# Cross attention: the low parts and the doubling of a tile's packed keys go from VectorE to GpSimd

## The chip, the core and the metric

The kernel runs on one core of one Trainium2 chip. The metric is the device time of one execution in microseconds (us); several runs are taken and their median is given. In the text PE is TensorE, DVE is VectorE, ACT is ScalarE, POOL is GpSimd and SP is the engine that issues the transfers from HBM.

## The reference

The program computes a small network of six layers on x of shape (2, 128, 256) with a context of shape (2, 2048, 256). The change lies in the first layer, a cross attention with 32 heads of 8 numbers:

```python
    k_raw = context @ Wk.T
    v_raw = context @ Wv.T
    ...
    q = _rmsnorm(q)
    k = _rmsnorm(k)
    scale = HEAD_DIM ** (-0.5)
    scores = jnp.einsum('bhnd,bhmd->bhnm', q, k) * scale
    attn = jax.nn.softmax(scores, axis=-1)
    out = jnp.einsum('bhnm,bhmd->bhnd', attn, v)
```

The fourth layer needs a weighted sum over the same context (a decaying scan whose mean is taken), so the kernel weighs each context tile while it is on the chip. The other layers (self attention, two feed-forward layers, a phase layer, experts) come afterwards and are not touched.

## The kernel before, in words

**Tiles.** The context is cut into 32 tiles of 128 rows (16 for each of two batches; `NB` is 32, `MB` is 16). Each tile t goes through the same steps on all engines, and a slot of most buffers is used by every second tile (`t % 2`).

**The way of a tile's keys.** POOL splits the context tile into an f16 high part and an f16 low part (`split_context`, lines L1694 and L1696). PE projects it into PSUM bank 7 (`project`, L1855). DVE takes the keys (`take_k`, L1563) and the values (`take_v`, L1570) out. POOL squares the keys (`square_keys`, L1687), DVE sums the squares of each head (`mean_squares`, L1576), ACT makes the reciprocal root by a logarithm and an exponential (`key_rstd`, L1795 and L1797). Then DVE makes the packed keys in `pack_keys`: the normalised keys `kn` (L1583), their f16 high part (L1590), the low part, that is `kn` minus the high part (L1592), and a doubling copy of 128x512 f16 (L1595). PE transposes the packed keys into bank 7 (`turn_keys`, L1867), DVE takes them out (`take_keys`, L1602). They are then used for the scores (L1884), ACT takes exponentials of the scores (L1805, four for each tile), and PE multiplies with the values (L1897).

**Weighing.** POOL multiplies each context tile with the decay weights (L1707) and adds the product to a sum (L1709) in `weigh_context`; for the first tile of a batch it is one multiplication (L1704).

**Order.** Each engine runs its own instruction list in the order in which the code is written, and semaphores join the lists. In its loop over t, DVE takes keys and values of tile t + 2, sums its squares, takes the transposed keys of tile t + 1, and then packs the keys of tile t + 2. POOL squares the keys of tile t, splits the context tile t + 2 and weighs tile t. For the second batch's queries POOL does some more at tiles 7 to 11 (`norm_q1` L1717, `high_q1` L1722, `low_q1` L1726), behind the weighing of the tile. SP loads a context tile into one of four slots when the weighing of four tiles before has freed it.

The buffers `kn` (128x256 f32, one slot), `kpack` (f16, two slots) and `ksq` are parts of the tile that the profile calls `sb_big`; `kraw`, `krs`, `kms` and the context tiles are parts of `sb_arena`; the split context lies in `sb_w_ri`.

Of the kernel before, what the change touches and what calls it, by code (L numbers as in the profile page):

```python
# [16 lines left out]
ALU = mybir.AluOpType  # L17
# [9 lines left out]
XH, XD = 32, 8  # L27
# [29 lines left out]
def build_program(nc, io):  # L57
    ctx = ExitStack()
    with ctx:
        sems = {}  # L60

        def sem(name):
            if name not in sems:
                sems[name] = ctx.enter_context(nc.semaphore(name))
            return sems[name]
# [87 lines left out]
        kn = big[:, 12800:13056]  # L153
        kpack = big[:, 13056:14080].bitcast(F16).rearrange("p (s n) -> p s n", s=2)
# [41 lines left out]
        for name, _, _ in loads:  # L196
            loaded[name] = loaded.get(name, 0) + 16
# [1293 lines left out]
        def pool_rest(pool):  # L1491
            G = nc.gpsimd
            pool_attention(pool)
            pool.wait_ge(sem("w_phase"), loaded["w_phase"])
            pool.wait_ge(sem("attn_out"), B)
            pool.wait_ge(sem("xf_low"), B)
            for kt in range(KT):
                for w in range(CONV):
                    G.tensor_tensor(w_cm[:, kt, w], w_mem[:, kt], w_conv[:, w], ALU.mult).then_inc(sem("w_cm_ready"), 1)
            for b in range(B):  # L1500

                pool.wait_ge(sem("summary_added"), b + 1)
                G.tensor_tensor(x[:, b], x[:, b], vecs[:, 2], ALU.add).then_inc(sem("beta_added"), 1)
            pool_scaled_units(pool)
            pool_phase(pool)
            pool_experts(pool)

        @block.vector
        def _(dve):
            V = nc.vector  # L1510
# [68 lines left out]
            def pack_keys(t):  # L1579

                dve.wait_ge(sem("k_rstd"), t + 1)
                knb = kn.rearrange("p (h d) -> p h d", d=XD)
                V.tensor_tensor(knb, kraw[:, t % 2].rearrange("p (h d) -> p h d", d=XD),  # L1583
                                krs[:, t % 2, :, None].to_broadcast([P, XH, XD]), ALU.mult
                                ).then_inc(sem("k_normed"), 1)
                if t >= 2:
                    dve.wait_ge(sem("k_transposed"), t - 1)
                dve.wait_ge(sem("k_normed"), t + 1)
                pack = kpack[:, t % 2].rearrange("p (h s r d) -> p h s r d", s=2, r=2, d=XD)
                V.tensor_copy(pack[:, :, 0, 0], knb).then_inc(sem("k_high"), 1)  # L1590
                dve.wait_ge(sem("k_high"), t + 1)
                V.tensor_tensor(pack[:, :, 0, 1], knb, pack[:, :, 0, 0], ALU.subtract).then_inc(sem("k_low"), 1)  # L1592
                dve.wait_ge(sem("k_low"), t + 1)
                halves_of = kpack[:, t % 2].rearrange("p (h s c) -> p h s c", s=2, c=16)
                V.tensor_copy(halves_of[:, :, 1], halves_of[:, :, 0]).then_inc(sem("k_packed"), 1)  # L1595

            def take_keys(t):

# [24 lines left out]
            take_v(0)  # L1623
            pack_q(0)
            pack_keys(0)
            mean_squares(1)
            take_keys(0)
            pack_keys(1)
            for t in range(NB):
                if t + 2 < NB:  # L1630
                    take_k(t + 2)
                    if t + 2 not in ACT_VALUES:
                        take_v(t + 2)
                    if t + 2 < MB:
                        decay_weights(t + 2)
                    else:
                        sum_weights(t + 2 - MB)
                    mean_squares(t + 2)
                if t + 1 < NB:
                    take_keys(t + 1)  # L1640
                if t + 2 < NB:
                    pack_keys(t + 2)
                if t == 4:
                    mean_squares_q(1)
# [36 lines left out]
        @block.gpsimd  # L1681
        def _(pool):
            G = nc.gpsimd

            def square_keys(t):
                pool.wait_ge(sem("k_taken"), t + 1)
                G.tensor_tensor(ksq[:, t % 2], kraw[:, t % 2], kraw[:, t % 2], ALU.mult).then_inc(sem("k_squared"), 1)  # L1687

            def split_context(t):

                pool.wait_ge(sem(f"ctx_loaded{t % CTX_SLOTS}"), 16 * (t // CTX_SLOTS + 1))
                if t >= 2:
                    pool.wait_ge(sem("kv_projected"), t - 1)
                G.tensor_copy(ctx_half[:, t % 2, 0], ctxT[:, t % CTX_SLOTS]).then_inc(sem("ctx_high"), 1)  # L1694
                pool.wait_ge(sem("ctx_high"), t + 1)
                G.tensor_tensor(ctx_half[:, t % 2, 1], ctxT[:, t % CTX_SLOTS], ctx_half[:, t % 2, 0],  # L1696
                                ALU.subtract).then_inc(sem("ctx_split"), 1)

            def weigh_context(t):

                pool.wait_ge(sem("geo_ready"), min(t + 1, MB))
                g = geo[:, None, (t % MB) * P:(t % MB + 1) * P].to_broadcast([P, KT, P])
                if t % MB == 0:
                    G.tensor_tensor(uacc[:, t // MB], ctxT[:, t % CTX_SLOTS], g, ALU.mult).then_inc(sem("ctx_weighted"), 1)  # L1704
                    return
                pool.wait_ge(sem("ctx_weighted"), t)
                G.tensor_tensor(gprod[:], ctxT[:, t % CTX_SLOTS], g, ALU.mult).then_inc(sem("ctx_weighed"), 1)  # L1707
                pool.wait_ge(sem("ctx_weighed"), t - t // MB)
                G.tensor_tensor(uacc[:, t // MB], uacc[:, t // MB], gprod[:], ALU.add).then_inc(sem("ctx_weighted"), 1)  # L1709

            qn1 = xn[:, 1].rearrange("p (h d) -> p h d", d=XD)
            pack1 = qpack[:, 1].rearrange("p (h s r d) -> p h s r d", s=2, r=2, d=XD)

            def norm_q1():
                pool.wait_ge(sem("q_rstd"), 2)
                pool.wait_ge(sem("q_copied"), 2)
                G.tensor_tensor(qn1, qraw[:, 1].rearrange("p (h d) -> p h d", d=XD),  # L1717
                                qrs[:, 1, :, None].to_broadcast([P, XH, XD]), ALU.mult).then_inc(sem("q1_normed"), 1)

            def high_q1(r):  # L1720
                pool.wait_ge(sem("q1_normed"), 1)
                G.tensor_copy(pack1[:, :, 0, r], qn1).then_inc(sem("q1_high"), 1)  # L1722

            def low_q1(r):
                pool.wait_ge(sem("q1_high"), r + 1)
                G.tensor_tensor(pack1[:, :, 1, r], qn1, pack1[:, :, 0, r], ALU.subtract).then_inc(sem("q1_packed"), 1)  # L1726

            split_context(0)
            split_context(1)
            weigh_context(0)  # L1730
            split_context(2)
            weigh_context(1)
            split_context(3)
            for t in range(2, NB):
                square_keys(t)
                if t + 2 < NB:
                    split_context(t + 2)
                weigh_context(t)
                if t == TURN_AT - 6:
                    norm_q1()  # L1740
                if TURN_AT - 5 <= t < TURN_AT - 3:
                    high_q1(t - TURN_AT + 5)
                if TURN_AT - 3 <= t < TURN_AT - 1:
                    low_q1(t - TURN_AT + 3)
            pool_rest(pool)
# [313 lines left out]
```

## Time and profile before

| | us |
|---|---|
| median of 3 runs | 408.24 |
| lowest and highest of them | 407.40, 408.91 |
| the profiled execution | 406.9 |
| its span, first to last instruction | 405.3 |
| PE, DVE, ACT, POOL busy in the span | 374.2, 329.2, 267.6, 221.5 |

The span is what the rows of a trace add up to; 1.6 us of the execution lie outside of it. The profiled execution is a single one, 1.3 us below the median of the three timed runs. A busy engine need not be the one that sets the end: PE is counted busy while its pipelined products drain.

### The profile page before, as it was taken

What the parts mean: (1) busy time and instruction counts of PE and PEld (TensorE: products, weight loads), DVE (VectorE), ACT (ScalarE), POOL (GpSimd) and SP (SyncE); (2) the same over time, 40 slices, a digit from 0 to 9 for tenths busy, and PEclk for the clock granted to TensorE, in tenths of its full rate; (3) what the DMA queues carried; (4) which work ended last, traced back from release to release, by engine and by line L of the source; (5) the groups of instructions that cost most, each with busy time, mean ns of one, the idle gap of its engine ahead of it and who ended that gap; (6) DMA issues with size and microseconds to landing.
All of it is one profiled execution on the core that took longest, in us unless ns stands there. A gap on an engine that the chain in (4) does not pass through costs nothing.

```text
span 405.3 us, 14183 instructions
## 1 busy us (share of the span) xinstructions
PE 374.2 (92%) x5863; PEld 288.4 (71%) x5863; DVE 329.2 (81%) x736; ACT 267.6 (66%) x554; POOL 221.5 (55%) x286
## 2 busy tenths in 40 slices
PE   7889989999999999889999999989889987799996
PEld 4456656666666767679989897778778864567775
DVE  7788989997799998768999996787997677866663
ACT  3588888897988898975545533822999246345532
POOL 2566577766566666016544430630399746999500
PEclk9999999999999999999999999999999999999999
DMA  5647641652311100570000017120000391000000
GB/s 165 234 136 247 225 140 44 185 158 69 113 40 38 35 25 4 158 287 2 2 0 2 1 46 313 32 112 1 2 2 2 123 392 62 2 1 2 2 0 27
DMA packets 10832, 34.77 MB, mean 86 GB/s; under 512 B 2193, under 2 KB 7313, under 8 KB 8977
## 3 DMA queue, kind: packets, MB, share of 16 engines
q1 hardware_dynamic: 10624, 33.86, 24.3%
q8 instruction: 47, 0.77, 0.7%
q14 instruction: 17, 0.13, 0.1%
q10 hardware_dynamic: 144, 0.00, 0.0%
HBM read 33.60 MB, written 0.26 MB: 84 GB/s over the span
## 4 chain that ended last, share of the span: by engine, by line
PE 51%; DVE 23%; POOL 10%; issue 9%; ACT 4%; DMA 1%; SPq 0%; DVEq 0%; POOLq 0%; ACTq 0%
PE ps L1897 9%; PE ps L1264 6%; PE ps L1855 5%; PE ps L1246 5%; PE ps L1884 3%; PE ps L1867 3%; PE ps L975 3%; PE ps L957 3%; PE ps L473 2%; PE ps L916 2%; POOL sb_w_ri L1696 2%; PE ps L923 2%; ACT sb_arena L1805 2%; DVE sb_big L654 2%; PE ps L534 1%
## 5 line engine op out<-in xcount | busy, mean ns | idle before, releaser
L1805 ACT ACTIVATE sb_arena<-ps 128x1024 f32<-128x1024 f32 x128 | 123.7, 1019 | 12.1 <-PE ps L1884 11.7
L1897 PE MATMUL ps<-sb_arena 128*25 128x128 f32 (+1 forms) x2048 | 68.7, 274 | 0.3 <-ACT sb_arena L1805 0.3
L1897 PEld LDWEIGHTS ps<-sb_arena 128*25 128x25 f32 (+1 forms) x2048 | 50.3, 97 | 7.5 <-ACT sb_arena L1805 1.0
L1855 PE MATMUL ps<-sb_w_ri 128*32 128x512 f16 x768 | 47.3, 379 | 3.0 <-DVE sb_arena L1602 1.8
L563 POOL TENSOR_TENSOR sb_halves<-sb_big,sb_halves 128x256 fp32r<-128x256 f32 x28 | 21.6, 792 | 43.7 <-ACT sb_halves L547 43.7
L1687 POOL TENSOR_TENSOR sb_big<-sb_arena 128x256 f32<-128x256 f32 x30 | 18.7, 623 | 45.3 <-DVE sb_arena L1563 45.3
L1855 PEld LDWEIGHTS ps<-sb_w_ri 128*32 128x32 f16 x768 | 21.5, 97 | 17.3 <-POOL sb_w_ri L1696 3.8
L1175 POOL TENSOR_TENSOR sb_mid<-sb_mid 128x512 f32<-128x512 f32 x16 | 21.9, 1376 | 20.3 <-DVE sb_mid L1075 20.2
L1338 ACT ACTIVATE sb_arena<-ps 128x176 f32<-128x176 f32 x40 | 12.5, 318 | 29.7 <-PE ps L1264 29.7
L1264 PE MATMUL ps<-sb_theta 128*128 128x352 f16 x168 | 26.9, 312 | 3.3 <-DVE sb_theta L1424 2.3
L1443 DVE SCALAR_TENSOR_TENSOR sb_arena<-ps,sb_w_q,sb_arena 128x176 f32<-128x176 f32 x40 | 15.4, 395 | 17.7 <-ACT sb_arena L1338 17.5
L1884 PEld LDWEIGHTS ps<-sb_w_ri,sb_arena 32*128 32x128 f16 x1024 | 14.9, 92 | 19.7 <-issue 14.8
L1884 PE MATMUL ps<-sb_w_ri,sb_arena 32*128 32x128 f16 x1024 | 25.8, 217 | 3.1 <-ACT sb_arena L1805 1.9
L473 PE MATMUL ps<-sb_halves 128*128 128x256 f32 x192 | 27.4, 292 | 0.7 <-DVE sb_halves L381 0.6
L1583 DVE TENSOR_TENSOR sb_big<-sb_arena 128x256 f32<-128x256 f32 x32 | 25.0, 781 | 3.3 <-ACT sb_arena L1797 2.7
L624 ACT ACTIVATE sb_arena<-sb_arena 128x128 f32<-128x128 f32 x32 | 12.6, 395 | 20.7 <-DVE sb_arena L692 20.7
L473 PEld LDWEIGHTS ps<-sb_halves 128*128 128x128 f32 x192 | 24.5, 190 | 2.2 <-issue 1.6
L1709 POOL TENSOR_TENSOR sb_uacc<-sb_uacc,sb_gprod 128x256 f32<-128x256 f32 x30 | 23.7, 790 | 2.4
L1602 DVE COPY sb_arena<-ps 128x1024 f16<-128x1024 f16 x32 | 22.0, 687 | 3.6 <-PE ps L1867 3.4
L1075 DVE SCALAR_TENSOR_TENSOR sb_mid<-ps,sb_w_nrm,sb_arena 128x1024 f32<-128x1024 f32 x16 | 20.5, 1283 | 5.3 <-PE ps L957 5.1
L1867 PE MATMUL ps<-sb_id,sb_big 128*128 128x128 f16 x256 | 19.7, 219 | 5.5 <-DVE sb_arena L1570 2.4
L1264 PEld LDWEIGHTS ps<-sb_theta 128*128 128x128 f16 x168 | 16.1, 98 | 12.0 <-DVE sb_arena L1443 1.9
(269 smaller groups left out, 929.6 us busy)
## 6 DMA issues: line engine op xcount, KB each, us to landing
sb_arena<-in_ctx SPq DMA_DIRECT2D x32, 128.0 KB, 2.6
sb_mid<-in_w_down SPq DMA_DIRECT2D x1, 3584.0 KB, 11.4
sb_big<-in_w_gu SPq DMA_DIRECT2D x1, 3520.0 KB, 11.1
sb_mid<-in_w_ffn SPq DMA_DIRECT2D x3, 768.0 KB, 5.2
sb_big<-in_w_gu SPq DMA_DIRECT2D x1, 2112.0 KB, 7.8
sb_big<-in_w_q SPq DMA_DIRECT2D x2, 1024.0 KB, 5.9
sb_big<-in_w_k SPq DMA_DIRECT2D x2, 1024.0 KB, 6.8
sb_big<-in_w_v SPq DMA_DIRECT2D x2, 1024.0 KB, 5.6
```

The costliest lines, as they stand in the source:

```text
L473: ins = T.matmul(ps[:, i % 2, w * 256:w * 256 + 256], qk_half[:, i % 2, c, w, kt], xa_half[:, d, kt], start=(n + kt == 0), stop=(n == 2 an ...
L563: ins = nc.gpsimd.tensor_tensor(qk_half[:, i % 2, 1, w], head_weights(i)[:, w], qk_half[:, i % 2, 0, w].bitcast(F32), ALU.subtract)
L1175: G.tensor_tensor(pa[:, j % 3, :, 0], pa[:, j % 3, :, 0], pa[:, j % 3, :, 1], ALU.add).then_inc(sem("out_summed"), 1)
L1264: i = T.matmul(ps[:, 2 + k % 4, 0:2 * EI], xe_half[:, c, kt, b * P:b * P + P], gu_half[u % 3][:, d, kt], start=(n + kt == 0), stop=(n == 2 ...
L1583: V.tensor_tensor(knb, kraw[:, t % 2].rearrange("p (h d) -> p h d", d=XD), krs[:, t % 2, :, None].to_broadcast([P, XH, XD]), ALU.mult).the ...
L1602: V.tensor_copy(kT[:, t % 2], ps[:, 7 if t else 5].bitcast(F16).rearrange("p (g m) -> p g m", g=GROUPS)).then_inc(sem("k_ready"), 1)
L1709: G.tensor_tensor(uacc[:, t // MB], uacc[:, t // MB], gprod[:], ALU.add).then_inc(sem("ctx_weighted"), 1)
L1805: nc.scalar.activation(probs[:, n % P_SLOTS].rearrange("p a g n -> p a (g n)"), ps[:, bank:bank + 2], ACT.Exp, scale=XD ** -0.5).then_inc( ...
L1855: i = T.matmul(ps[r:r + 32, 7], ctx_half[:, t % 2, c, kt, r:r + 32], wkv_half[:, d, kt], start=(n + kt == 0), stop=(n == 2 and kt == KT - ...
L1867: i = T.transpose(out[:, g * P:(g + 1) * P], kpack[:, t % 2, g * P:(g + 1) * P], id16[:])
L1884: i = T.matmul(ps[:, 2 * (n % 3) + j % 2, gg * P:(gg + 1) * P], kT[rows, t % 2, 4 * half + gg], qT_x[rows, t // MB, 4 * half + gg], start= ...
L1897: i = T.matmul(ps[32 * gg:32 * gg + m, 6, j * P:(j + 1) * P], v_sb[:, t % V_SLOTS, 4 * gg + j, head], probs[:, n % P_SLOTS, a, gg], start= ...
```

## The change

The last two of the four packing steps leave DVE's `pack_keys` and become a function `finish_keys` on POOL. In POOL's loop it stands behind the splitting of tile t + 2 and ahead of the weighing of tile t; for tiles 0 and 1 it stands around the splitting of tile 3. Since `kn` has one slot, DVE now waits, before it normalises the keys of tile t, until POOL has made the low part of tile t - 1.

```diff
             def pack_keys(t):
 
                 dve.wait_ge(sem("k_rstd"), t + 1)
+                if t >= 1:
+                    dve.wait_ge(sem("k_low"), t)
...
                 V.tensor_copy(pack[:, :, 0, 0], knb).then_inc(sem("k_high"), 1)
-                dve.wait_ge(sem("k_high"), t + 1)
-                V.tensor_tensor(pack[:, :, 0, 1], knb, pack[:, :, 0, 0], ALU.subtract).then_inc(sem("k_low"), 1)
-                dve.wait_ge(sem("k_low"), t + 1)
-                halves_of = kpack[:, t % 2].rearrange("p (h s c) -> p h s c", s=2, c=16)
-                V.tensor_copy(halves_of[:, :, 1], halves_of[:, :, 0]).then_inc(sem("k_packed"), 1)
...
+            def finish_keys(t):
+
+                pool.wait_ge(sem("k_high"), t + 1)
+                pack = kpack[:, t % 2].rearrange("p (h s r d) -> p h s r d", s=2, r=2, d=XD)
+                G.tensor_tensor(pack[:, :, 0, 1], kn.rearrange("p (h d) -> p h d", d=XD), pack[:, :, 0, 0], ALU.subtract
+                                ).then_inc(sem("k_low"), 1)
+                pool.wait_ge(sem("k_low"), t + 1)
+                halves_of = kpack[:, t % 2].rearrange("p (h s c) -> p h s c", s=2, c=16)
+                G.tensor_copy(halves_of[:, :, 1], halves_of[:, :, 0]).then_inc(sem("k_packed"), 1)
...
             weigh_context(1)
+            finish_keys(0)
             split_context(3)
+            finish_keys(1)
             for t in range(2, NB):
                 square_keys(t)
                 if t + 2 < NB:
                     split_context(t + 2)
+                finish_keys(t)
                 weigh_context(t)
```

Line numbers move: on POOL the squaring is L1684 in the changed kernel, the split L1701 and L1703, the weighing L1714 and L1716, and the two new instructions are L1690 and L1694.

On POOL, before, the list from the first squaring to the second one reads so (tiles 2 and 3; `sb_big` as output is the square of the keys, `sb_w_ri` the split context, `sb_gprod` and `sb_uacc` the weighing):

```order
L1687 TENSOR_TENSOR sb_big<-sb_arena 128x256
L1694 CAST sb_w_ri<-sb_arena 128x256
L1696 TENSOR_TENSOR sb_w_ri<-sb_arena,sb_w_ri 128x256
L1707 TENSOR_TENSOR sb_gprod<-sb_arena,sb_w_q 128x256
L1709 TENSOR_TENSOR sb_uacc<-sb_uacc,sb_gprod 128x256
L1687 TENSOR_TENSOR sb_big<-sb_arena 128x256
```

The same place in the changed kernel:

```order
L1684 TENSOR_TENSOR sb_big<-sb_arena 128x256
L1701 CAST sb_w_ri<-sb_arena 128x256
L1703 TENSOR_TENSOR sb_w_ri<-sb_arena,sb_w_ri 128x256
L1690 TENSOR_TENSOR sb_big<-sb_big 128x32x8
L1694 COPY sb_big<-sb_big 128x32x16
L1714 TENSOR_TENSOR sb_gprod<-sb_arena,sb_w_q 128x256
L1716 TENSOR_TENSOR sb_uacc<-sb_uacc,sb_gprod 128x256
L1684 TENSOR_TENSOR sb_big<-sb_arena 128x256
```

The low part and the doubling of tile t now stand between the split and the weighing, so the weighing of tile t and the squaring of tile t + 1 stand behind them.

On DVE, before, one turn of the loop reads so, from the sum of squares of one tile to that of the next (`ps` to `sb_arena` 128x1024 is `take_keys`, 128x256 is `take_k`, `sb_w_q` the decay weights):

```order
L1576 TENSOR_REDUCE sb_arena<-sb_big 128x32
L1602 COPY sb_arena<-ps 128x1024
L1583 TENSOR_TENSOR sb_big<-sb_arena 128x256
L1590 CAST sb_big<-sb_big 128x32x8
L1592 TENSOR_TENSOR sb_big<-sb_big 128x32x8
L1595 COPY sb_big<-sb_big 128x32x16
L1563 COPY sb_arena<-ps 128x256
L1530 SCALAR_TENSOR_TENSOR sb_w_q<-sb_dec,sb_w_q,sb_ones 128x128
L1576 TENSOR_REDUCE sb_arena<-sb_big 128x32
```

The same turn in the changed kernel:

```order
L1576 TENSOR_REDUCE sb_arena<-sb_big 128x32
L1599 COPY sb_arena<-ps 128x1024
L1585 TENSOR_TENSOR sb_big<-sb_arena 128x256
L1592 CAST sb_big<-sb_big 128x32x8
L1563 COPY sb_arena<-ps 128x256
L1530 SCALAR_TENSOR_TENSOR sb_w_q<-sb_dec,sb_w_q,sb_ones 128x128
L1576 TENSOR_REDUCE sb_arena<-sb_big 128x32
```

Two instructions of the turn are gone; the rest stands in the same order.

## Rows read from the trace of the kernel before

**Rows 1.** page of the profile, its first line
```profile
span 405.3 us, 14183 instructions
```

**Rows 2.** windows, from the first to the last squaring of keys
```profile
20.72:160.20 139.48, 132.25 (x3667) 91.20 (x3661) 124.08 (x286) 122.25 (x184) 92.72 (x148) 1.00 0.34 106
```

**Rows 3.** chain that ended last, by line, in 24 to 35 and 75 to 86 us
```profile
by line: issue 39.0%; POOL sb_uacc L1709 21.7%; POOL sb_big L1687 18.6%; POOL sb_gprod L1707 12.8%; POOL sb_w_ri L1696 12.2%; POOL sb_w_ri L1694 6.2%; POOLq L1693 0.5%; POOLq L1706 0.3%
by line: PE ps L1897 36.3%; PE ps L1855 23.5%; PE ps L1867 16.6%; PE ps L1884 13.6%; issue 4.1%; DVE sb_arena L1570 3.7%; DVE sb_arena L1563 3.0%
```

**Rows 4.** line L1687 (squaring of keys); duration ns min/median/max, first and last start
```profile
L1687 POOL TENSOR_TENSOR sb_big<-sb_arena x30: 612/613/719, 20.7 to 160.2; 128x256 f32<-128x256 f32 x30
```

**Rows 5.** timeline of one tile: start us, us, engine, line
```profile
75.35 0.61 POOL L1687 TENSOR_TENSOR sb_big<-sb_arena 128x256 f32<-128x256 f32 x1 [1.35 <-DVE sb_arena L1563]
75.90 0.53 POOL L1694 CAST sb_w_ri<-sb_arena 128x256 f16<-128x256 f32 x1
76.27 0.42 DVE L1576 TENSOR_REDUCE sb_arena<-sb_big 128x32 f32<-128x256 f32 x1
76.51 0.67 POOL L1696 TENSOR_TENSOR sb_w_ri<-sb_arena,sb_w_ri 128x256 f16<-128x256 f32 x1
76.61 0.68 DVE L1602 COPY sb_arena<-ps 128x1024 f16<-128x1024 f16 x1
77.14 0.73 POOL L1707 TENSOR_TENSOR sb_gprod<-sb_arena,sb_w_q 128x256 f32<-128x256 f32 x1
77.25 0.90 DVE L1583 TENSOR_TENSOR sb_big<-sb_arena 128x256 f32<-128x256 f32 x1
77.95 0.79 POOL L1709 TENSOR_TENSOR sb_uacc<-sb_uacc,sb_gprod 128x256 f32<-128x256 f32 x1
78.25 0.64 DVE L1590 CAST sb_big<-sb_big 128x256 f16<-128x256 f32 x1
78.93 0.42 DVE L1592 TENSOR_TENSOR sb_big<-sb_big 128x256 f16<-128x256 f32 x1
79.39 0.29 DVE L1595 COPY sb_big<-sb_big 128x512 f16<-128x512 f16 x1
79.60 0.42 DVE L1563 COPY sb_arena<-ps 128x256 f32<-128x256 f32 x1
80.09 0.61 POOL L1687 TENSOR_TENSOR sb_big<-sb_arena 128x256 f32<-128x256 f32 x1 [1.35 <-DVE sb_arena L1563]
```

**Rows 6.** timeline, the same DVE lines with POOL idle
```profile
157.85 0.42 DVE L1583 TENSOR_TENSOR sb_big<-sb_arena 128x256 f32<-128x256 f32 x1
158.38 0.29 DVE L1590 CAST sb_big<-sb_big 128x256 f16<-128x256 f32 x1
```

**Rows 7.** POOL lines L1726, L1722, L1694, L1319; columns as in rows 4
```profile
L1726 POOL TENSOR_TENSOR sb_theta<-sb_xn,sb_theta x2: 717/717/717, 63.8 to 68.9; 128x256 f16<-128x256 f32 x2
L1722 POOL CAST sb_theta<-sb_xn x2: 460/462/463, 54.1 to 58.9; 128x256 f16<-128x256 f32 x2
L1694 POOL CAST sb_w_ri<-sb_arena x32: 389/398/593, 7.5 to 151.8; 128x256 f16<-128x256 f32 x32
L1319 POOL CAST sb_w_ri<-sb_mid x12: 609/609/1345, 338.2 to 378.7; 128x512 f16<-128x512 f32 x12
```

**Rows 8.** timeline of the start and of tile 7, POOL and DVE
```profile
14.88 0.73 POOL L1696 TENSOR_TENSOR sb_w_ri<-sb_arena,sb_w_ri 128x256 f16<-128x256 f32 x1
20.72 0.72 POOL L1687 TENSOR_TENSOR sb_big<-sb_arena 128x256 f32<-128x256 f32 x1 [5.11 <-DVE sb_arena L1563]
21.54 0.42 DVE L1576 TENSOR_REDUCE sb_arena<-sb_big 128x32 f32<-128x256 f32 x1 [0.51 <-POOL sb_big L1687]
50.28 0.63 POOL L1717 TENSOR_TENSOR sb_xn<-sb_theta,sb_qrs 128x256 f32<-128x256 f32 x1 [2.13 <-ACT sb_qrs L1771]
```

**Rows 9.** timeline, ACT at the end of the cross attention
```profile
161.84 0.23 ACT L1795 ACTIVATE sb_arena<-sb_arena 128x32 f32<-128x32 f32 x1
170.02 1.94 ACT L1805 ACTIVATE sb_arena<-ps 128x1024 f32<-128x1024 f32 x2 [0.33 <-PE ps L1897]
```

## The prediction, made before the changed kernel was run

> **What bounds the kernel now.** I read the windows first, for the stretch that the change touches: from the first squaring of keys on POOL (tile 2) to the last (tile 31). The columns of [rows 2] are the stretch's length and then the busy time of PE, PEld, DVE, ACT and POOL. The stretch is 139.5 us of a span of 405.3 [rows 1], and in it DVE is busy for 124.1, ACT for 122.3 and POOL for 92.7. No engine is full except by its share of PE's pipelined time, so what sets the pace must be a loop between engines. There are 30 squarings, so 29 steps [rows 4]: 139.5 / 29 = 4.81 us for a tile on average. The chain, read next, shows that no engine holds this pace alone: early on it runs through POOL and "issue", later almost wholly through PE [rows 3]. Then the timeline of one tile [rows 5], from one squaring (75.35) to the next (80.09), 4.74 us. The reader is to see two things there. POOL's five instructions end at 78.74 and POOL then waits 1.35 us for the next keys. DVE goes from sum of squares to normalising, high part, low part, doubling and the next keys with hardly a gap.
>
> It looks as if DVE were the engine to relieve and POOL the one with room. What counts, though, is where POOL's room lies. It lies behind the weighing, and the new instructions stand ahead of it.
>
> **The change, part by part.** *Removed from DVE*: a low part of 0.42 and a doubling of 0.29 [rows 5], 0.71 us a tile, or 32 x 0.71 = 22.7 us in all.
>
> *Added to POOL*: a low part and a doubling for each of 32 tiles. The low part has a near twin before: L1726 does the same subtraction in the same strided shape for a query tile, 0.72 us [rows 7]. The doubling (128x512 f16 to f16) has none. From below: the cast of 256 elements, 0.39, which would be its price if bytes counted. From above: L1319, the cast of 512 elements, which mostly takes 0.61 but reaches 1.35. The strided cast L1722 costs 0.46 where the plain L1694 costs 0.39 to 0.40 [rows 7]. Elements are the same in L1319, and strides add some 0.06, so I take 0.66. Together 1.38 us on POOL for 0.71 on DVE.
>
> A page speaks against such a move: the Trainium skill, "GPSIMD Engine Reference", sections "Elementwise — side-by-side cycle accounting" and "Engine selection", says that elementwise work belongs on VectorE, with GpSimd about half as fast on two inputs and near line rate on one. The rows agree on the direction (0.72 against 0.42). By the page's 2.6 cycles an element for two inputs and 1.03 for one at 1.2 GHz, I estimate 0.55 and 0.44 us without the start of an instruction, 0.39 less than my sum, which would take some 11 us off the forecast.
>
> *The new order*. On POOL the list of a tile is now squaring t, split t + 2, low part t, doubling t, weighing t, squaring t + 1. The low part waits for DVE's high part of tile t. That high part needs the normalised keys, these need the root, the root needs the sum of squares, and this needs POOL's squaring of the same tile, one step earlier in POOL's own list. And the squaring of t + 1 is queued behind the weighing of t. Before, POOL waited for keys only; now it stops in the middle of each tile until DVE and ACT have gone round, and the weighing no longer lies beside that round. So the steps form one ring:
>
> - squaring 0.61 [rows 5], hand-over to DVE 0.10 (20.72 + 0.72 to 21.54) [rows 8]: 0.71
> - DVE from the start of the sum of squares to the start of normalising, with the transposed keys between, 76.27 to 77.25: 0.98 [rows 5]. The root on ACT lies beside it.
> - normalising and high part: in [rows 5] 0.90 and 0.64, beside POOL's weighing; in [rows 6], with POOL idle, 157.85 to 158.67: 0.82. In the ring POOL's split ends about 1.15 after the squaring (cast 0.40, product 0.67, a gap of 0.08), the normalising starts about 1.08 after it, and the high part falls where POOL can do nothing but wait for it. So I take 0.82.
> - hand-over to POOL 0.07 (79.60 + 0.42 to 80.09) [rows 5], low part 0.72, gap 0.08, doubling 0.66: 1.53
> - weighing 77.14 to 78.74: 1.60 [rows 5]; its start and the next squaring's overlap their neighbours by 0.04 each: 1.52
>
> Sum 0.71 + 0.98 + 0.82 + 1.53 + 1.52 = 5.56 us a tile. Nothing hides it: PE's work of a tile fits (its chain ran at 4.7), and ACT's is four exponentials at 0.97 and two small ones at 0.23 [rows 9], 4.34. Both now wait for the ring.
>
> 29 steps are 161.2 us. The query work at tiles 7 to 11 stands behind the weighing, thus in the ring: 0.63 [rows 8], twice 0.46 and twice 0.72 [rows 7], 3.0, less overlaps 2.8. Before, POOL waited there 2.13 for ACT [rows 8]; ACT's root for it is ready sooner than the longer ring gets there, so nothing is added. DVE's scan of the decay weights, in the first half, falls beside the weighing now; beside the split's cast it cost POOL 0.53 - 0.40 [rows 5, 7], so some 0.1 x 14 = 1.4. New stretch 165.4, that is 25.9 more.
>
> Ahead of it, tiles 0 and 1 are finished in POOL's gap of 5.11 between 15.61 and 20.72 [rows 8]: two times 1.46 and the waits for DVE's high parts just fit, +0.2. Behind it, ten exponentials follow the last root (161.84 to 171.96) [rows 9]; that tail keeps its length. Sum: 25.9 + 0.2 = +26.1. The profiled execution took 406.9, so 433.0; the median of the runs before is 1.3 above it: **434 us**.
>
> Bounds of the ring: low part at a plain product's 0.61 (the squaring) and doubling at 0.39 give 5.18 and, without the scan's share, 421. The doubling at 1.35 gives 6.25 and 454.
>
> **The rivals.**
>
> *DVE relieved, faster.* If the ring did not close, DVE's turn would shrink by 0.71 below ACT's 4.34, and 29 x (4.81 - 4.34) = 13.6 us would go: 395. For it: DVE is the fullest of DVE, ACT and POOL in the stretch, and normalising beside an idle POOL takes 0.42 instead of 0.90. Against it: the order on POOL. Without low part and doubling the ring is 5.56 - 1.53 = 4.03, so the point that decides is whether the two, with hand-over and gap, cost under 0.78; their cheapest rows give 0.61 + 0.39 + 0.15 = 1.15.
>
> *Hidden anyway.* Keys are packed about a tile ahead of their scores, so a single delay would be absorbed and the time stay at 408. Against it: the delay comes again with every tile, since each squaring waits for the weighing ahead of it.
>
> *The cheap ends* of both POOL instructions: 421, still slower.
>
> *Contention.* If the normalising meets the split's product, it takes 0.90, and the ring grows by 0.48: 29 x 0.48 = 13.9, so 448; a doubling beside a busy DVE gives up to 454. For it: the margin is under 0.1 us (1.08 against 1.15). Against it: the tail of one instruction is all that is left to collide with.
>
> **How the numbers follow.** The ring as summed, 424 to 447: 0.74. Contention, 447 to 460: 0.10. Cheap ends, 420 to 424: 0.08. Hidden: 0.03. Faster: 0.05. The range 420 to 447 holds 0.82. Half a per cent, 2 us, is about what a measurement of this kernel can tell from no change; slower by more 0.92, within 0.03, faster by more 0.05.
>
> **What would show it.** Squarings on POOL 5.5 us apart instead of 4.8. POOL waiting in front of the low part for DVE's L1592, and no longer in front of the squaring. DVE waiting in front of its sum of squares for POOL, some 1.5 us a tile. Normalising near 0.42 and high part near 0.29 in most tiles. The exponentials L1805 with more idle time in front of them. After the last exponential nothing changed. It would be wrong if POOL's doubling were far from 0.66, if the squarings came again at 4.7, or if PE, with small gaps in every tile, ran at a lower granted clock than the 1.00 of [rows 2].

## The result and the profile after

The change makes the kernel slower: 426.79 us (425.42 to 426.91) against 407.82 (406.98 to 408.91) in four runs each, a ratio of 1.046 with a 95% interval of 1.043 to 1.048. Forecast were 434 us and a range of 420 to 447. The profiled execution took 426.9.

The first lines of the page of the changed kernel, with PE's busy time:

```profile
span 425.3 us, 14214 instructions
PE 379.9 (89%) x5863; PEld 287.0 (67%) x5863; DVE 285.5 (67%) x672; ACT 269.6 (63%) x554; POOL 257.9 (61%) x350
```

The span is 20.0 us longer than before [rows 1]; the medians differ by 19.0, since the profiled execution of the kernel before was 0.9 below its median and that of the changed kernel is at it. Where the 20.0 us lie is read from the windows, again from the first squaring of keys to the last (length, then busy PE, PEld, DVE, ACT, POOL, granted clock, DMA):

```profile
21.84:180.92 159.08, 138.51 (x3713) 90.83 (x3713) 83.78 (x230) 125.70 (x185) 125.40 (x205) 1.00 0.30 93
```

The same 29 steps take 159.1 us instead of 139.5 [rows 2], 5.49 a tile instead of 4.81. So 19.6 of the 20.0 us lie in this stretch. DVE has 40 us less to do in it and POOL 33 more. POOL is the only engine with a larger share of the stretch than before, 79% instead of 66%, and PE, the fullest, has fallen from 95% to 87%. It is not a full engine that costs the time.

The lines of the squaring, the two new POOL instructions and the two packing steps left on DVE (x count: ns min/median/max, first and last start):

```profile
L1684 POOL TENSOR_TENSOR sb_big<-sb_arena x30: 609/613/716, 21.8 to 180.9; 128x256 f32<-128x256 f32 x30
L1690 POOL TENSOR_TENSOR sb_big<-sb_big x32: 669/673/677, 15.7 to 183.4; 128x256 f16<-128x256 f32 x32
L1694 POOL COPY sb_big<-sb_big x32: 609/610/612, 16.4 to 184.2; 128x512 f16<-128x512 f16 x32
L1585 DVE TENSOR_TENSOR sb_big<-sb_arena x32: 411/426/427, 14.8 to 182.5; 128x256 f32<-128x256 f32 x32
L1592 DVE CAST sb_big<-sb_big x32: 293/294/296, 15.3 to 183.1; 128x256 f16<-128x256 f32 x32
```

Both POOL instructions came in under their price, 0.67 and 0.61 us. Normalising and high part on DVE take 0.43 and 0.29 in every tile; before they took 0.90 and 0.64, as in [rows 5], in most tiles (these are the medians).

One tile of the timeline, POOL and DVE, from one squaring to the next (start, us):

```profile
79.08 0.61 POOL L1684 TENSOR_TENSOR sb_big<-sb_arena 128x256 f32<-128x256 f32 x1
79.64 0.39 POOL L1701 CAST sb_w_ri<-sb_arena 128x256 f16<-128x256 f32 x1
79.79 0.42 DVE L1576 TENSOR_REDUCE sb_arena<-sb_big 128x32 f32<-128x256 f32 x1 [1.83 <-POOL sb_big L1684]
80.11 0.67 POOL L1703 TENSOR_TENSOR sb_w_ri<-sb_arena,sb_w_ri 128x256 f16<-128x256 f32 x1
80.13 0.68 DVE L1599 COPY sb_arena<-ps 128x1024 f16<-128x1024 f16 x1
80.77 0.43 DVE L1585 TENSOR_TENSOR sb_big<-sb_arena 128x256 f32<-128x256 f32 x1
81.30 0.29 DVE L1592 CAST sb_big<-sb_big 128x256 f16<-128x256 f32 x1
81.67 0.67 POOL L1690 TENSOR_TENSOR sb_big<-sb_big 128x256 f16<-128x256 f32 x1 [0.89 <-DVE sb_big L1592]
82.41 0.61 POOL L1694 COPY sb_big<-sb_big 128x512 f16<-128x512 f16 x1
82.48 0.42 DVE L1563 COPY sb_arena<-ps 128x256 f32<-128x256 f32 x1 [0.89 <-PE ps L1865]
82.82 0.48 DVE L1570 COPY sb_arena<-ps 128x128 f32<-128x128 f32 x2
82.98 0.73 POOL L1714 TENSOR_TENSOR sb_gprod<-sb_arena,sb_w_q 128x256 f32<-128x256 f32 x1
83.22 0.77 DVE L1530 TENSOR_TENSOR_SCAN sb_w_q<-sb_dec,sb_w_q,sb_ones 128x128 f32<-128x128 f32 x1
83.79 0.72 POOL L1716 TENSOR_TENSOR sb_uacc<-sb_uacc,sb_gprod 128x256 f32<-128x256 f32 x1
84.47 0.61 POOL L1684 TENSOR_TENSOR sb_big<-sb_arena 128x256 f32<-128x256 f32 x1
```

The reader is to follow it as a ring. POOL squares (79.08) and splits the next context tile, then stands still from 80.78 for 0.89 us, until DVE, which has summed the squares and taken the transposed keys meanwhile, has normalised and made the high part. Then POOL makes low part and doubling and weighs, with no gap above 0.08 us, and only then squares the next tile's keys (84.47). DVE meanwhile stands still in front of each sum of squares, for 1.83 us here and for 46.0 / 30 = 1.5 us on average. Each engine waits for the other once a tile. The waits of the cross attention say the same, in total us, times and the longest:

```profile
DVE sb_arena L1576 <- POOL sb_big L1684: 46.0, 30, 2.6
POOL sb_big L1690 <- DVE sb_big L1592: 29.3, 30, 2.0
...
ACT sb_arena L1805 <- DVE sb_arena L1576: 23.8, 27, 1.5
```

POOL's wait before was in front of the squaring, for new keys [rows 5]; it is now in front of the low part. And the chain that ended last, from 120 to 131 us, is the ring itself, where the chain of the kernel before was 90% PE's work from 75 to 86 us [rows 3]:

```profile
by line: POOL sb_big L1690 18.4%; POOL sb_big L1694 16.6%; POOL sb_uacc L1716 13.2%; POOL sb_gprod L1714 12.6%; DVE sb_arena L1599 12.4%; POOL sb_big L1684 10.5%; issue 10.4%; DVE sb_big L1585 7.2%; DVE sb_big L1592 5.6%; DVE sb_arena L1576
```

### The profile page after: what moved, and what is told of

It is laid out like the page before. It is cut to its first block, busy times and chain, and to the rows that moved or that the text cites. A ratio compares the mean times of both kernels' runs of the same rounds, so it can differ in the third digit from the quotient of the medians.

```text
span 425.3 us, 14214 instructions
## 1 busy us (share of the span) xinstructions
PE 379.9 (89%) x5863; PEld 287.0 (67%) x5863; DVE 285.5 (67%) x672; ACT 269.6 (63%) x554; POOL 257.9 (61%) x350
## 4 chain that ended last, share of the span: by engine, by line
PE 32%; DVE 28%; POOL 25%; issue 8%; ACT 4%; DMA 1%; DVEq 0%; POOLq 0%; SPq 0%; ACTq 0%
PE ps L1264 5%; POOL sb_uacc L1716 5%; POOL sb_gprod L1714 4%; POOL sb_big L1690 4%; PE ps L1246 4%; POOL sb_big L1694 4%; DVE sb_arena L1599 4%; POOL sb_big L1684 4%; DVE sb_big L1585 3%; PE ps L975 3%; PE ps L957 2%; PE ps L473 2%; DVE sb_big L1592 2%; PE ps L916 2%; PE ps L1907 2%
## 5 line engine op out<-in xcount | busy, mean ns | idle before, releaser
L1907 PE MATMUL ps<-sb_arena 128*25 128x128 f32 (+1 forms) x2048 | 69.7, 275 | 0.5 <-ACT sb_arena L1815 0.3
L1865 PE MATMUL ps<-sb_w_ri 128*32 128x512 f16 x768 | 48.7, 386 | 20.5 <-DVE sb_arena L1599 10.8
L1865 PEld LDWEIGHTS ps<-sb_w_ri 128*32 128x32 f16 x768 | 20.1, 96 | 41.6 <-POOL sb_w_ri L1703 26.9
L1576 DVE TENSOR_REDUCE sb_arena<-sb_big 128x32 f32<-128x256 f32 x32 | 13.4, 420 | 46.0 <-POOL sb_big L1684 46.0
L1690 POOL TENSOR_TENSOR sb_big<-sb_big 128x256 f16<-128x256 f32 x32 | 21.5, 673 | 31.3 <-DVE sb_big L1592 31.3
L1563 DVE COPY sb_arena<-ps 128x256 f32<-128x256 f32 x30 | 12.7, 425 | 27.8 <-PE ps L1865 27.8
L1703 POOL TENSOR_TENSOR sb_w_ri<-sb_arena,sb_w_ri 128x256 f16<-128x256 f32 x32 | 22.3, 698 | 2.6
```

The source lines that it names most:

```text
L1690: G.tensor_tensor(pack[:, :, 0, 1], kn.rearrange("p (h d) -> p h d", d=XD), pack[:, :, 0, 0], ALU.subtract).then_inc(sem("k_low"), 1)
L1865: i = T.matmul(ps[r:r + 32, 7], ctx_half[:, t % 2, c, kt, r:r + 32], wkv_half[:, d, kt], start=(n + kt == 0), stop=(n == 2 and kt == KT - ...
L1907: i = T.matmul(ps[32 * gg:32 * gg + m, 6, j * P:(j + 1) * P], v_sb[:, t % V_SLOTS, 4 * gg + j, head], probs[:, n % P_SLOTS, a, gg], start= ...
```

## The experiments

All were timed together with the kernel before, whose median was 407.7 to 407.8 us in these runs.

**1. Low part and doubling behind the weighing.** The same instructions on the same engine, with two lines of POOL's loop exchanged:

```diff
-                finish_keys(t)
                 weigh_context(t)
+                finish_keys(t)
```

Expected: 

> In POOL's loop the low part and the doubling of tile t stand behind the weighing of tile t instead of ahead of it; nothing else differs from the changed kernel. Ring theory (what costs is that the weighing stands in one ring with the squaring, the root, the high part, the low part and the doubling): the weighing then lies beside DVE's round, which in turn slows to some 0.90 and 0.64 for normalising and high part, so a tile takes 0.61 + 0.10 + 0.98 + 1.64 + 1.35 = about 4.7 us instead of 5.4, and the kernel 404 to 413 us. Rival 1 (POOL is simply the slower engine for these two instructions, wherever they stand): no change from the changed kernel, 427. Rival 2 (the time from a tile's squaring to its packed keys is what costs): that way gets longer, 435 to 445.

Measured: 410.51 us (410.21 to 410.67), ratio to the kernel before 1.006, interval 1.004 to 1.008. That is 16.3 us below the changed kernel with the very same work on POOL. So where the two instructions stand explains most of the loss, and the first rival falls; the second, that the way from squaring to packed keys costs, falls too, since that way is longer here (from the start of the squaring to the end of the doubling 4.75 us, 131.67 to 136.42, against 3.94 in the changed kernel, 79.08 to 83.02). The timeline shows the price of the order: POOL's product (L1714) and DVE's normalising (L1585) now start beside each other, and the one that starts second takes longer. Two pieces, one of the first half and one of the second:

```profile
63.50 0.73 POOL L1714 TENSOR_TENSOR sb_gprod<-sb_arena,sb_w_q 128x256 f32<-128x256 f32 x1
63.53 0.98 DVE L1585 TENSOR_TENSOR sb_big<-sb_arena 128x256 f32<-128x256 f32 x1
...
131.67 0.61 POOL L1684 TENSOR_TENSOR sb_big<-sb_arena 128x256 f32<-128x256 f32 x1
133.29 0.42 DVE L1585 TENSOR_TENSOR sb_big<-sb_arena 128x256 f32<-128x256 f32 x1
133.33 0.97 POOL L1714 TENSOR_TENSOR sb_gprod<-sb_arena,sb_w_q 128x256 f32<-128x256 f32 x1
136.38 0.61 POOL L1684 TENSOR_TENSOR sb_big<-sb_arena 128x256 f32<-128x256 f32 x1
```

Squarings 4.71 us apart are POOL's own work now: in the windows of this kernel, from 105 to 150.5 us, POOL (the fifth busy time) is busy for 41.7 of 45.5.

```profile
105.00:150.50 45.50, 43.70 (x1225) 30.00 (x1217) 29.61 (x78) 41.31 (x61) 41.69 (x66) 1.00 0.18 53
```

**2. Only the doubling on POOL**, in the place of the change. The low part goes back to DVE:

```diff
             def pack_keys(t):
...
                 V.tensor_copy(pack[:, :, 0, 0], knb).then_inc(sem("k_high"), 1)
+                dve.wait_ge(sem("k_high"), t + 1)
+                V.tensor_tensor(pack[:, :, 0, 1], knb, pack[:, :, 0, 0], ALU.subtract).then_inc(sem("k_low"), 1)
...
             def finish_keys(t):
 
-                pool.wait_ge(sem("k_high"), t + 1)
...
-                G.tensor_tensor(pack[:, :, 0, 1], kn.rearrange("p (h d) -> p h d", d=XD), pack[:, :, 0, 0], ALU.subtract
-                                ).then_inc(sem("k_low"), 1)
                 pool.wait_ge(sem("k_low"), t + 1)
```

Expected: 

> Only the doubling is on POOL, in the same place between split and weighing; the low part is back on DVE. Ring theory: the ring loses POOL's low part with its gap (0.74) and gains DVE's (0.46), so 0.28 a tile, 29 times: about 8 us below the changed kernel, 417 to 420. Rival (the low part, with its DVE wait on one slot of normalised keys, is the cause): back to 407 to 409. Rival (any stop of POOL for DVE in the middle of a tile costs the same): 427.

Measured: 418.44 us (418.29 to 419.85), ratio 1.027, interval 1.023 to 1.030: 8.35 us below the changed kernel. The timeline shows the ring at 5.04 us (from 130.40 to 135.44), 0.28 less than the changed kernel's 5.32 in this part:

```profile
129.34 0.43 DVE L1594 TENSOR_TENSOR sb_big<-sb_big 128x256 f16<-128x256 f32 x1
129.83 0.61 POOL L1692 COPY sb_big<-sb_big 128x512 f16<-128x512 f16 x1 [1.26 <-DVE sb_big L1594]
130.40 0.74 POOL L1712 TENSOR_TENSOR sb_gprod<-sb_arena,sb_w_q 128x256 f32<-128x256 f32 x1
...
134.87 0.61 POOL L1692 COPY sb_big<-sb_big 128x512 f16<-128x512 f16 x1 [1.26 <-DVE sb_big L1594]
135.44 0.73 POOL L1712 TENSOR_TENSOR sb_gprod<-sb_arena,sb_w_q 128x256 f32<-128x256 f32 x1
```

Neither the low part alone nor any stop of POOL as such is the cause; the time follows the length of the ring.

**3. The low part twice.** The second one writes the same values again:

```diff
-                G.tensor_tensor(pack[:, :, 0, 1], kn.rearrange("p (h d) -> p h d", d=XD), pack[:, :, 0, 0], ALU.subtract
-                                ).then_inc(sem("k_low"), 1)
-                pool.wait_ge(sem("k_low"), t + 1)
+                for r in range(2):
+                    G.tensor_tensor(pack[:, :, 0, 1], kn.rearrange("p (h d) -> p h d", d=XD), pack[:, :, 0, 0], ALU.subtract
+                                    ).then_inc(sem("k_low"), 1)
+                    pool.wait_ge(sem("k_low"), 2 * t + r + 1)
```

DVE's wait counts to 2 * t accordingly.

Expected: 

> The changed kernel with POOL's low part made twice over (the second writes the same values again). Ring theory: each of the 29 steps grows by the whole 0.74 us, 21 to 23 us with the two tiles of the start, so 448 to 450. Rival (POOL is busy for only 61% of the span and has room for it): under 5 us, 427 to 432.

Measured: 450.33 us (450.28 to 450.38, two runs), ratio 1.104, interval 1.100 to 1.108, which is 23.5 above the changed kernel. The line of the low part:

```profile
L1691 POOL TENSOR_TENSOR sb_big<-sb_big x64: 667/672/676, 15.7 to 205.8; 128x256 f16<-128x256 f32 x64
```

One low part with its gap is 0.74 us (81.67 to 82.41 in the timeline above). The stretch from the first squaring to the last, 22.03 to 202.51, is 180.5 us long instead of 159.1, 21.4 more, and 29 x 0.74 is 21.5. So every us added on POOL at this place is paid in full, though POOL is busy for only 61% of the changed kernel's span. The other 2 us are not the ring's: 1.8 of them lie behind the last squaring, where PE's mean granted clock is 0.86 for 12 us (1.00 in the changed kernel).

**4. The squaring ahead of the weighing.** POOL's loop is turned:

```diff
+            square_keys(2)
             for t in range(2, NB):
-                square_keys(t)
                 if t + 2 < NB:
                     split_context(t + 2)
                 finish_keys(t)
+                if t + 1 < NB:
+                    square_keys(t + 1)
                 weigh_context(t)
```

Expected: 

> POOL's loop is turned: split t + 2, low part and doubling of t, squaring of t + 1, weighing of t. So the squaring of the next tile no longer waits for the weighing. Ring theory: the weighing (1.5 us) leaves the ring, DVE's round lies beside weighing and split and is slowed by them, and what is left is POOL's own work of about 4.6 us a tile or the ring at about 4.7: 404 to 411 us. Rival 1 (POOL is the slower engine, wherever the instructions stand): 427. Rival 2 (moving work off DVE is worth its 0.71 us a tile once the ring is gone): 395.

Measured: 412.85 us (410.01 to 414.13), ratio 1.011, interval 1.006 to 1.017. Taking the weighing out of the ring gives back 13.9 of the 19.0 us, so the ring theory holds, but the time lies 2 us above the top of what it expected. From 110 us on its squarings come 4.67 us apart, as expected; in the first half most steps are still 5.1 to 6.0 us. The waits show a new stop, in front of DVE's taking of the keys (L1563), for PE's projection, and behind it POOL's squaring; the first was 27.8 us in the changed kernel too, but nothing in POOL's list waited for it there but once:

```profile
DVE sb_arena L1563 <- PE ps L1867: 26.7, 29, 2.1
...
POOL sb_big L1684 <- DVE sb_arena L1563: 4.6, 7, 1.1
```

**5. Doubling only, squaring ahead** (edits 2 and 4 together; DVE's wait for `k_low` is dropped, since POOL reads no `kn`).

Expected: 

> Both ways of easing the ring together: POOL makes only the doubling (the low part is back on DVE, so DVE doesn't wait for POOL's low part either), and in POOL's loop the squaring of t + 1 stands behind the doubling of t and ahead of the weighing of t. POOL's work of a tile falls to about 3.9 us and the ring under 4.7. Ring theory: PE's own work of a tile, 4.6 us by the chain of the kernel before, sets the pace, 404 to 410 us. Rival (what is left on POOL still costs its difference to DVE, 0.3 us a tile): 415 to 418.

Measured: 409.22 us (406.83 to 411.30, 12 runs), ratio 1.003, interval 1.001 to 1.006. Inside the range of the ring theory, but no gain over the kernel before. Two neighbouring POOL rows show the squaring waiting for keys that have not been taken yet:

```profile
44.65 0.61 POOL L1690 COPY sb_big<-sb_big 128x512 f16<-128x512 f16 x1 [0.68 <-DVE sb_big L1592]
47.07 0.61 POOL L1684 TENSOR_TENSOR sb_big<-sb_arena 128x256 f32<-128x256 f32 x1 [1.81 <-DVE sb_arena L1563]
```

Between a squaring and the next split there now stands the weighing, so the split of a later tile, its projection and the taking of its keys come later after a squaring than before. That the late split is what holds PE up here was not tried by a run of its own.

**6. Doubling only, behind the weighing** (edits 1 and 2 together, again without the wait for `k_low` on DVE).

Expected: 

> As the kernel with low part and doubling behind the weighing, but POOL makes only the doubling; DVE keeps the low part and has no new wait. Ring theory: POOL's work of a tile is 3.9 us instead of 4.6 and DVE's turn is 0.29 shorter than in the kernel before; the first half of the tiles, where DVE sets the pace of the kernel before, gains some 0.1 to 0.2 us a tile, the second half, where PE does, nothing: 404 to 407 us, just under the kernel before. Rival (any of this work on POOL costs): 410 or more.

Measured: 404.96 us (404.79 to 405.74), ratio 0.994, interval 0.9915 to 0.9961. This version beats both kernels, the one before by 2.9 us. Its stretch from the first squaring to the last, in the columns used above:

```profile
20.50:158.30 137.80, 132.79 (x3669) 91.08 (x3661) 115.74 (x257) 122.16 (x184) 109.13 (x176) 1.00 0.35 107
```

137.8 us instead of 139.5. In the second half, from 110 to 150 us, the chain runs through PE alone:

```profile
by line: PE ps L1903 44.9%; PE ps L1861 29.1%; PE ps L1890 15.0%; PE ps L1873 11.2%
```

The gain doesn't lie where it was expected. Tile 16 is squared at 89.73 in the kernel before and at 89.22 here:

```profile
89.73 0.61 POOL L1687 TENSOR_TENSOR sb_big<-sb_arena 128x256 f32<-128x256 f32 x1 [1.49 <-DVE sb_arena L1563]
89.22 0.61 POOL L1684 TENSOR_TENSOR sb_big<-sb_arena 128x256 f32<-128x256 f32 x1
```

Up to there the 14 steps of the first half take 69.0 and 68.7 us, and the 15 behind it 70.5 and 69.1. So the second half, which was to gain nothing, has 1.4 of the 1.7 us, and that the time lies in the expected range is luck in part. The kernel before has a chain of PE's work there too (98.6% from 110 to 150 us), with squarings 4.62 us apart; here they are 4.52 apart. Its PE was still held a little: it starts to transpose 0.10 us after DVE has taken the values out of the same bank (132.61 + 0.47 to 133.18), here 0.31 after it (131.16 + 0.48 to 131.95).

**7. Low part and doubling left out.** The kernel before, whose DVE makes low part and doubling for tiles 0 and 1 only; all later tiles keep those in their slots:

```diff
+                if t >= 2:
+                    V.tensor_copy(pack[:, :, 0, 0], knb).then_inc(sem("k_packed"), 1)
+                    return
                 V.tensor_copy(pack[:, :, 0, 0], knb).then_inc(sem("k_high"), 1)
```

Expected: 

> The kernel before with low part and doubling left out on every engine for tiles 2 to 31 (the slots keep those of tiles 0 and 1): what DVE's relief is worth if nobody has to do the work. Theory that PE's own 4.6 us a tile stands close behind DVE: only the first half gains, 3 to 5 us, 402 to 406. Rival (each 0.71 us on DVE counts until ACT's 4.34 a tile is reached): 394 to 397.

Measured: 403.57 us (402.96 to 405.36), ratio 0.990, interval 0.988 to 0.993. If nobody had to do this work, the kernel would gain 4.3 us. Here both halves gain: the stretch is 4.0 us shorter than before, 2.6 of it in the first 14 steps and 1.4 in the last 15. The chain from 110 to 150 us is PE's here too:

```profile
by line: PE ps L1900 44.1%; PE ps L1858 29.1%; PE ps L1887 14.6%; PE ps L1870 12.4%
```

In this half the squarings of experiments 5, 6 and 7 come mostly 4.51 to 4.52 us apart, however much DVE and POOL have to do in each. So PE's own work sets that step.

## Why the prediction was right, and where its sizes were off

**The mechanism** was right: POOL's list and DVE's close into a ring, because the squaring of t + 1 is queued behind the weighing of t, and that behind low part and doubling, which wait for DVE. Experiments 1 and 4 take the weighing out of the ring in two ways and give back 16.3 and 13.9 us; experiment 3 lengthens the ring by 0.74 and is paid one to one in the stretch (21.4); experiment 2 shortens it by 0.28, where 29 x 0.28 is 8.1, and gains 8.35, 7.5 of them in the stretch and the rest ahead of it, where PE kept its clock (1.00 from 19.5 to 22.5 us, 0.50 in the changed kernel).

**The ring** was put at 5.56 us and is 5.39 in the first half (79.08 to 84.47) and 5.32 in the second, where squaring and hand-over take 0.65 instead of 0.71:

```profile
127.66 0.61 POOL L1684 TENSOR_TENSOR sb_big<-sb_arena 128x256 f32<-128x256 f32 x1
132.98 0.61 POOL L1684 TENSOR_TENSOR sb_big<-sb_arena 128x256 f32<-128x256 f32 x1
```

The largest term that was too high is that of the two instructions: from the end of the high part to the start of the weighing it is 81.59 to 82.98, 1.39 for 1.53. The low part took 0.67 for 0.72 (its twin before was the query's), the doubling 0.61 for 0.66: the strides cost nothing here, and its price is that of the 512-element cast, the median of [rows 7]. The weighing, 82.98 to 84.47, is 1.49 for 1.52; squaring and hand-over, DVE's 0.98, and normalising with high part, 0.82, are as said in the tile at 79.08. Over 14 steps of 0.17 and 15 of 0.23 these differences make 5.8 of the 6.3 us by which the stretch came out below 165.4.

The estimate that I took from the Trainium skill, "GPSIMD Engine Reference", section "Elementwise — side-by-side cycle accounting", for the two instructions without their start was 0.99 us (0.55 and 0.44). Measured were 1.28, so it was 0.29 too low where my 1.38 was 0.10 too high. The kernel time by it, 423, was 4 us low, mine 7 us high.

**Single tiles** differ, in ways that I had not counted. That they about cancel is luck: with the query work they add 3.7 us to the ring as measured, where 4.2 were forecast. DVE's scan beside the weighing was put at 0.1 in each of 14 tiles, 1.4. It made POOL's product longer in the first two only (0.90 and 0.85), and in the others DVE's scan took the delay. The first two steps, 6.02 and 5.52, are the longest without query work in the first half. Tile 16 has one weighing instruction instead of two (a step of 4.53 us), and the change of batch behind it costs a step of 6.48 (6.19 in the kernel before).

**The start** was put at +0.2 and is +1.1. Here PE's clock is the reason: in the profile of experiment 1, whose POOL and DVE lists are the same up to there, the clock stayed at full and the first squaring is at 20.93, the forecast +0.2; see the last section. The tail behind the last squaring got 0.7 shorter, where no change was expected. The 1.3 us that I added for the way from the profiled execution to the median didn't come: in the changed kernel these two are the same within 0.1.

**The rivals.** Contention was priced at 448 and didn't come: the longest normalising is 0.427 us, though in the trace it starts up to about 0.08 us before the split's product ends. "Hidden anyway" fell as it was argued, since the delay comes again with every tile. For the faster rival I gave the right reason against (the two instructions with hand-over and gap cost 1.39, not under 0.78), but a wrong price: I let the tile shrink to ACT's 4.34 us and put 13.6 us on it. Experiment 7 shows 4.3 us. Next behind DVE stands PE, with 4.51 us a tile in the second half (experiments 5 to 7). The second row of [rows 3] had its chain, nearly without other work in it, and I had named its pace, yet I didn't use it as the floor.

**What was to be seen**: squarings 5.5 us apart, POOL's wait in front of the low part, DVE's 1.5 us in front of its sum of squares: all are there. One sign was wrong: the exponentials have no more idle time in front of them than before (9.9 us in all against 12.1). ACT's new idle time, 24 us, stands in front of the logarithm of the key's root, since that is what comes in its list when the sum of squares is late.

## What to carry to other kernels

Before moving work to an engine with room, find where in its list the room lies. Write down the ring: which instruction waits for the other engine, and what is queued behind it that the other engine will wait for next. If the sum of the ring exceeds the present step, the difference is paid in every step, however idle both engines look. The same two instructions cost 19 us ahead of an independent piece of work and 3 behind it. And before pricing a relief, look for the next engine in the chain: here it left 4 us of a hoped-for 14.

## What the runs showed of the hardware

**Who starts first wins.** In experiment 1, DVE's normalising (two inputs from SBUF, the on-chip memory) and POOL's product start within 0.04 us of each other. Where POOL's started first (63.50), it took 0.73 and DVE's took 0.98; where DVE's did (133.29), it took 0.42 and POOL's took 0.97. Either alone takes 0.42 and 0.73. So the second ends 0.28 us (DVE) or 0.59 us (POOL) behind the first, 0.14 less than it takes alone: most of it comes after the first has ended. The Trainium skill, "SBUF — State Buffer", section "SBUF: two separate sides", says that VectorE with two inputs there and GpSimd share a pair of ports as an exclusive lock, held for the whole instruction by whichever starts first; these rows agree with it.

**PE's clock at the start.** In the profiled execution of the changed kernel PE ran at half its clock (1.2 of 2.4 GHz) for some 3 us (columns as above, the granted clock third from the end):

```profile
16.00:19.50 3.50, 1.80 (x39) 1.08 (x40) 1.32 (x3) 1.79 (x4) 2.31 (x5) 0.97 1.00 393
19.50:22.50 3.00, 3.00 (x52) 1.14 (x44) 0.82 (x2) 1.25 (x4) 1.59 (x3) 0.50 0.03 11
```

In the kernel before, the same place, the clock stayed at full:

```profile
16.00:19.50 3.50, 1.76 (x40) 1.12 (x44) 2.88 (x8) 2.05 (x4) 0.00 (x0) 1.00 0.90 349
19.50:22.50 3.00, 2.17 (x56) 1.14 (x44) 1.77 (x4) 2.12 (x7) 1.70 (x4) 1.00 0.03 11
```

The busy time of PE just ahead of it is nearly the same in both (1.80 and 1.76 us of 3.5). The projection in this stretch took 2.39 us where the same one in experiment 1 took 1.48 at full clock; the first line is the changed kernel's, the second that of experiment 1:

```profile
18.89 2.39 PE L1865 MATMUL ps<-sb_w_ri 128*32 128x512 f16 x24
18.89 1.48 PE L1865 MATMUL ps<-sb_w_ri 128*32 128x512 f16 x24
```

That explains 0.9 of the 1.1 us at the start. Of the four timed runs of the changed kernel the three with a mean granted clock of 0.996 took 426.7 to 426.9 us, the one with 1.000 took 425.4. The fall happened in the profile of experiment 7 too, and not in that of experiment 1; what decides it isn't settled by these runs.
